# Layer 3's self attention: values and sums one turn earlier in the software pipeline

## The chip, the cores and the metric

The kernel runs on one core of a Trainium2 chip. The metric is the device time of one execution in microseconds; times are given as the median over runs. TensorE (PE in the profile, PEld its weight loads), VectorE (DVE), ScalarE (ACT) and GpSimd (POOL) each run their own instructions in order and wait for each other by semaphores.

## The reference

The program is a decoder of four layers, each a token mixer, a cross attention and a feed-forward part, each followed by a residual and a layer norm. It works on 16 sequences of 128 tokens with 256 channels. The change touches only the token mixer of layer 3, a self attention with 16 heads of 16 channels and a penalty on each pair of positions:

```python
def _L3_attn_ref(hidden_states, Wq, bq, Wk, bk, Wv, bv, Wg, bg):
    ...
    log_pen = jnp.log(jnp.maximum(penalties, 1e-32))
    ...
    q = split_heads(hidden_states @ Wq + bq)
    k = split_heads(hidden_states @ Wk + bk)
    v = split_heads(hidden_states @ Wv + bv)
    scores = jnp.einsum('bhqd,bhkd->bhqk', q, k) / np.sqrt(HEAD_DIM)
    scores = scores + log_pen[:, None, :, :]
    probs = jax.nn.softmax(scores, axis=-1)
    ctx = jnp.einsum('bhqk,bhkd->bhqd', probs, v)
    ctx = ctx.transpose(0, 2, 1, 3).reshape(b, s, h)
    return ctx
```

The result is added to x and layer-normalised: `x = _layernorm(x + _L3_attn_ref(...))`.

## The kernel before

The kernel holds the 16 blocks of 128 tokens (one sequence each, NB = 16) in SBUF from stage to stage. One function, `attention16`, serves four attentions: the cross attentions of layers 1, 2 and 3 and the self attention of layer 3. Only the last passes a `penalty` (a table of weights by which the exponentials are multiplied), and `own=True` (keys and values come from x itself). Its buffers appear in the profile with the prefix `a_` (and those of layer 3's cross attention, which follows it, with `x_`).

The function is a software pipeline written out by hand. Every engine runs over the same `TURNS`, n = -1, 0, 1, ...; in each turn it works on several blocks at different depths, and a block's number is n minus a fixed distance. `LAG` is the distance of the values and sums (`attend_values`, `attend_sums`), and the steps behind them stand at LAG + 1, LAG + 2 and LAG + 3. With the penalty LAG is 2, without it 1. In turn n, for layer 3's self attention:

- TensorE: `scores(n, 0)` (scores of block n, first half of the heads, for the maxima, in pR; interleaved with the scores of block n-1, second half, the right way round for the exponentials, in pT), `turn_back(n-LAG-3)`, `output(n-LAG-2)` (transposes for this attention), `scores(n, 1)`, `projections(n+1)`, `maxima(n)` (two transposes of the maxima), `attend_values(n-LAG)` and `attend_sums(n-LAG)` (32 matmuls each, line 2073).
- ScalarE: the exponentials of block n-1 (both halves), the copy of the turned-back x, then queries, value and key of block n+1.
- VectorE: `maximum(n, 0)`, `residual(n-LAG-2)`, `normalise(n-LAG-1)`, `maximum(n, 1)`, `put_maxima(n)` (the maxima go into spare rows of the queries; it waits for TensorE's `maxima(n)`), `spread(n-LAG-2)`, then the two weighings `weigh(n-1, 1)` and `weigh(n-1, 0)` (exponentials times penalty, line 2265), and `scaled(n-LAG-2)`.
- GpSimd: adds the bias to the values of block n+1 and writes them to a buffer of V; the power of the norm, the store of x and the residual's copy.

`attend_values(b)` waits for both weighings of block b:

```python
def attend_values(b):
    since(pe, w_done[0], b)
    since(pe, w_done[1], b)
    since(pe, v_stored, b)
    since(pe, oT_ready, b - 1)
```

`since(eng, event, b)` waits until the event has happened for block b. With LAG = 2 those are the weighings that VectorE did in the turn before. V has LAG + 2 buffers; the weights Pr have two (block parity).

Of the kernel before, what the change touches and what calls it, by code (L numbers as in the profile page):

```python
# [1838 lines left out]
def attention16(core, a, name, early, bq=False, bv=False, bo=False, own=False, rope=False, mask=None, penalty=None,  # L1839
# [3 lines left out]
    with Stage(core, name) as s:  # L1843
        SCALE = float(DH) ** -0.5
        LIFT = 60.0
        SLOTS16 = KD * PAIR
        LAG = 2 if penalty is not None else 1
        TURNS = range(-1, NB + LAG + 3)
        KV = core.XT if own else core.CT
        moved = bq and not rope  # L1850
# [24 lines left out]
        kx = [s.sb(f"kx{i}", [P, SLOTS16, P]) for i in range(4)]  # L1875
        V = [s.sb(f"V{i}", [P, H16, ROWS]) for i in range(LAG + 2)]
        mx = s.sb("mx", [P, KD, P])
# [42 lines left out]
        def live(b):  # L1920

            return 0 <= b < NB
# [17 lines left out]
        def _(pool):  # L1940
# [13 lines left out]
            def sum_k(b):  # L1954
                since(pool, k_turned, b)
                since(pool, k_stored, b - 1)
                pool.tensor_tensor(k32[:], rk[0][:], rk[1][:], ALU.add).then_inc(k_summed, 1)
# [7 lines left out]
            def residual(b):  # L1965
                since(pool, y_used, b - 1)
                if bo:
                    pool.tensor_tensor(xres[:], core.X[:, b, :], bot[:], ALU.add).then_inc(xres_ready, 1)
                else:
                    pool.tensor_copy(xres[:], core.X[:, b, :]).then_inc(xres_ready, 1)  # L1970

            def root(b):
                since(pool, ve_ready, b)
                pool.tensor_tensor(rstd[:], ve[:], core.mhalf[:], ALU.pow).then_inc(rstd_ready, 1)  # L1974

            def store(b):
                since(pool, xn_ready, b)
                pool.tensor_copy(core.X[:, b, :], xn[:]).then_inc(x_stored, 1)

            for n in TURNS:  # L1980
# [4 lines left out]
                if rope and live(n + 1):  # L1985
                    sum_k(n + 1)
                if live(n - LAG - 2):
                    root(n - LAG - 2)
                    store(n - LAG - 2)
                if live(n - LAG - 1):  # L1990
                    residual(n - LAG - 1)
# [340 lines left out]
def l1_xattn(core, a, after):  # L2332
    attention16(core, a, "x1", core.x1, bq=True, bv=True, bo=True, rope=True, after=[*after, core.a2])
# [38 lines left out]
def l2_xattn(core, a, mask, lists, values):  # L2372
    attention16(core, a, "x2", core.x2, bo=True, mask=(mask.out, mask.back), after=[lists, core.a3, core.pen],
                kv=(core.keys2, values))


def l3_xattn(core, a, tables, values):
    attention16(core, a, "x3", core.x3, bo=True, after=[tables], kv=(core.keys3, values))
# [1838 lines left out]
```

## Time and profile before

| | |
|---|---|
| median of 3 runs | 2903.16 us (2898.19 to 2906.47) |
| the profiled execution | 2894.84 us, of which the span of the trace is 2892.9 us |
| granted TensorE clock, mean over the span | 0.914 |
| TensorE, VectorE, ScalarE, GpSimd busy | 83%, 49%, 29%, 23% of the span |
| the stage of layer 3's self attention | from about 2154 to 2345 us |

The profile lists instructions with the line of the kernel, what they write and read, and the idle time of the engine ahead of them with what released it. The granted clock is the share of TensorE's full 2.4 GHz that it was given; 0.50 is 1.2 GHz.

### The profile page before, as it was taken

The numbers are of one execution on the slowest core, as the hardware profiler recorded it, in microseconds if no ns is written. First come the engines' busy times: TensorE is split into PE (matmuls) and PEld (weight loads), VectorE is DVE, ScalarE is ACT, GpSimd is POOL, SyncE is SP. The second block draws the span as 40 slices with busy tenths as digits, with TensorE's granted clock in tenths as the row PEclk, the third lists the DMA queues.
The fourth block names the chain that finished last, engine by engine and source line by source line (L and its number), as shares of the span: only waits on it lengthen the run. The fifth ranks groups of instructions, "written<-read, shape, count | busy, mean of one in ns | idle before, by whom it ended". The sixth has DMA issues, their size and how long they took to land. (4 is left out here: it accounts for less than half of the span.)

```text
span 2892.9 us, 53588 instructions
## 1 busy us (share of the span) xinstructions
PE 2415.0 (83%) x20563; PEld 1900.2 (66%) x20565; DVE 1421.9 (49%) x2899; ACT 847.3 (29%) x1462; POOL 676.6 (23%) x1011
## 2 busy tenths in 40 slices
PE   7869999568889899899889979729887869499990
PEld 3847777334578665799778856518656657399980
DVE  3256666576458631121267747551167958611115
ACT  1123333453234311011122224302245525122220
POOL 1932222231123200122112201102212212123331
PEclk8979999888989999999999989959889979799995
DMA  9020000100020000688500020015400000289982
GB/s 339 6 78 1 0 0 1 30 0 0 1 83 2 31 1 0 254 311 322 199 16 0 0 81 2 31 45 146 129 1 2 3 4 3 90 286 325 325 278 89
DMA packets 163710, 254.27 MB, mean 88 GB/s; under 512 B 17760, under 2 KB 124512, under 8 KB 163296
## 3 DMA queue, kind: packets, MB, share of 16 engines
q1 hardware_dynamic: 154336, 230.98, 23.1%
q0 software_dynamic: 9216, 21.06, 2.7%
q8 instruction: 114, 1.87, 0.3%
q14 instruction: 44, 0.36, 0.0%
HBM read 220.35 MB, written 31.13 MB: 87 GB/s over the span
## 5 line engine op out<-in xcount | busy, mean ns | idle before, releaser
L3180 PE MATMUL te_pU<-te_xsT,te_wu 128*128 128x128 f32 x1952 | 235.6, 278 | 1.6 <-DVE te_xsT L3260 1.6
L3180 PEld LDWEIGHTS te_pU<-te_xsT,te_wu 128*128 128x128 f32 x1952 | 233.0, 195 | 5.4 <-issue 2.4
L3201 PE MATMUL te_pY<-te_wd,te_hT 128*128 128x256 f32 x976 | 220.8, 379 | 0.0
L3201 PEld LDWEIGHTS te_pY<-te_wd,te_hT 128*128 128x128 f32 x976 | 180.7, 190 | 22.0
L2252 DVE TENSOR_REDUCE x_mx<-x_pR 128x8 f32<-128x1024 f32 x96 | 117.4, 1223 | 74.5 <-PE x_pR L2042 71.5
L2167 ACT ACTIVATE x_Pr<-x_pT 128x1024 f32<-128x1024 f32 x96 | 97.9, 1020 | 169.5 <-PE x_pT L2047 169.5
L1117 PE MATMUL x_pB<-early,x_xlT 128*128 128x384 f32 x384 | 137.5, 502 | 4.7 <-DVE x_qn L1344 3.0
L2042 PE MATMUL x_pR<-x_kx,x_qx 32*128 32x128 f32 x1536 | 118.4, 293 | 22.3 <-ACT x_kx L2200 13.8
L2042 PEld LDWEIGHTS x_pR<-x_kx,x_qx 32*128 32x128 f32 x1536 | 100.3, 196 | 51.2 <-issue 45.8
L3221 ACT ACTIVATE te_hT<-te_pU 128x512 f32<-128x512 f32 x78 | 46.6, 597 | 242.4 <-PE te_pU L3180 242.4
L2047 PE MATMUL x_pT<-x_qx,x_kx 32*128 32x128 f32 x1536 | 115.6, 289 | 1.4 <-ACT x_Pr L2167 1.2
L3239 DVE COPY te_ys<-te_pY 128x256 f32<-128x256 f32 x61 | 25.9, 425 | 162.8 <-PE te_pY L3201 162.8
L3234 DVE TENSOR_TENSOR te_hT<-te_pU,te_sg 128x512 f32<-128x512 f32 x44 | 30.4, 692 | 149.4 <-ACT te_sg L3219 149.4
L1117 PEld LDWEIGHTS x_pB<-early,x_xlT 128*128 128x128 f32 x384 | 71.1, 195 | 47.8 <-issue 5.4
L3219 ACT ACTIVATE te_sg<-te_pG 128x512 f32<-128x512 f32 x44 | 26.3, 597 | 251.4 <-PE te_pG L3180 251.4
L2047 PEld LDWEIGHTS x_pT<-x_qx,x_kx 32*128 32x128 f32 x1536 | 96.9, 192 | 3.2 <-ACT x_Pr L2167 1.7
L3236 DVE COPY te_xsT<-te_pT 128x256 f32<-128x256 f32 x61 | 25.7, 421 | 134.5 <-PE te_pT L3174 134.5
L1974 POOL TENSOR_TENSOR x_rstd<-x_ve,mhalf 128x1 f32<-128x1 f32 x48 | 26.3, 549 | 277.6 <-DVE x_ve L2291 277.6
L3180 PE MATMUL te_pG<-te_xsT,te_wg 128*128 128x128 f32 x704 | 86.0, 275 | 0.0
L2301 DVE RECIPROCAL x_R<-x_pO 128x256 f32<-128x256 f32 x48 | 83.9, 1748 | 0.5 <-PE x_pO L2073 0.5
L3180 PEld LDWEIGHTS te_pG<-te_xsT,te_wg 128*128 128x128 f32 x704 | 82.5, 193 | 0.0
L2000 PE MATMUL x_pq<-XT,early 128*128 128x128 f32 x512 | 78.1, 308 | 5.2 <-PEq L284 3.0
(618 smaller groups left out, 5601.3 us busy)
## 6 DMA issues: line engine op xcount, KB each, us to landing
te_wu<-in_L_ffn_w_upT SPq DMA_DIRECT2D x39, 1024.0 KB, 5.6
te_wd<-in_L_ffn_w_downT SPq DMA_DIRECT2D x39, 1024.0 KB, 5.7
te_wu<-in_L_ffn_up SPq DMA_DIRECT2D x22, 1024.0 KB, 5.0
te_wg<-in_L_ffn_gate SPq DMA_DIRECT2D x22, 1024.0 KB, 7.0
te_wd<-in_L_ffn_down SPq DMA_DIRECT2D x22, 1024.0 KB, 7.8
moe_first<-in_L_ffn_W SPq DMA_DIRECT2D x8, 1024.0 KB, 8.6
ao_got<-ys_slots SPq DMA_DIRECT2D x12, 512.0 KB, 6.1
xs_slots<-zeros SPq DMA_DIRECT2D x1, 5120.0 KB, 23.5
```

Of the source, the lines that this page charges most:

```text
L1117: ins = pe.matmul(pB[:, n, 0:HALF], xlT[t][:, src + k, :], w[:, k, bass.ts(n, HALF)], start=(k == 0), stop=(k == KD - 1))
L1974: pool.tensor_tensor(rstd[:], ve[:], core.mhalf[:], ALU.pow).then_inc(rstd_ready, 1)
L2000: ins = pe.matmul(out[:, t, :], ws[t // KD][:, k, bass.ts(t % KD, P)], src[:, k, bass.ts(b, P)], start=(k == 0), stop=(k == KD - 1))
L2042: return pe.matmul(pR[:, j, c, :], qx[b % 4][g, c, :], kx[b % 4][g, c, :], start=mask is None, stop=mask is None or c == SLOTS16 - 1)
L2047: return pe.matmul(pT[:, j, c, :], kx[b % 4][g, c, :], qx[b % 4][g, c, :], start=mask is None, stop=mask is None or c == SLOTS16 - 1)
L2167: ins = act.activation(Pr[b % 2][half][:], pT[:], ACT.Exp, scale=SCALE)
L2252: dve.tensor_reduce(out, pR[:].rearrange("p j (i t) n -> p (j i) t n", i=PAIR), AX.X, ALU.max).then_inc(mx_ready[half], 1)
L2301: dve.reciprocal(R[:], pO[:, 1, :, :]).then_inc(o_inverted, 1)
L3180: ins = pe.matmul(out[g][:, m, :], w[:, k, bass.ts(PER * g + m, P)], xsT[:, k, :], start=(k == 0), stop=(k == KD - 1))
L3201: ins = pe.matmul(pY[u][:, 0, :], hT[:, k, :], wd[u][:, k, :], start=(k == 0), stop=(k == KH - 1))
L3221: act.activation(hT[:, PER * g:PER * (g + 1), :], pU[g][:], act_fn).then_inc(h_done, 1)
L3234: dve.tensor_tensor(hT[:, PER * g:PER * (g + 1), :], pU[g][:], sg[g][:], ALU.mult).then_inc(h_done, 1)
```

## The change

LAG is 1 for every caller. In layer 3's self attention the values and sums of a block are then asked for in the turn in which VectorE weighs its exponentials (block n-1 in turn n), output, residual, normalising and turning back come one turn sooner, V has three buffers instead of four, and the loop has one turn less (n goes to 19 instead of 20). The order of the steps within a turn is unchanged on every engine, as are all computations. The other three attentions stay the same.

```diff
-        LAG = 2 if penalty is not None else 1
+        LAG = 1
         TURNS = range(-1, NB + LAG + 3)
```

## Rows read from the trace of the kernel before

**Rows 1.** Busy time by windows: engine busy us (instructions), granted clock, DMA share, GB/s

```profile
core 0: us, PE busy (x) PEld busy (x) DVE busy (x) ACT busy (x) POOL busy (x), PEclk, DMA share, GB/s
2154.00:2345.30 191.30, 143.18 (x2464) 122.37 (x2464) 145.34 (x213) 92.27 (x192) 47.43 (x70) 0.91 0.01 2
2172.40:2182.90 10.50, 7.01 (x86) 6.24 (x86) 4.53 (x5) 5.40 (x11) 0.72 (x1) 0.84 0.01 2
...
2223.70:2309.95 86.25, 72.84 (x1386) 62.22 (x1386) 79.39 (x118) 51.99 (x109) 26.43 (x36) 1.00 0.01 2
...
2312.40:2315.40 3.00, 0.00 (x1) 0.01 (x1) 2.89 (x3) 1.11 (x1) 0.00 (x0) 1.00 0.01 3
2315.90:2319.30 3.40, 3.40 (x67) 2.93 (x66) 3.18 (x6) 0.00 (x0) 1.46 (x1) 0.56 0.00 0
...
2327.70:2331.10 3.40, 0.03 (x1) 0.00 (x0) 3.00 (x5) 0.22 (x1) 0.12 (x1) 0.71 0.00 0
```

**Rows 2.** Timeline of VectorE, one steady turn: start us, us

```profile
2242.89 1.22 DVE L2252 TENSOR_REDUCE a_mx<-a_pR 128x8 f32<-128x1024 f32 x1
...
2247.04 1.22 DVE L2252 TENSOR_REDUCE a_mx<-a_pR 128x8 f32<-128x1024 f32 x1
2248.80 0.88 DVE L2259 SCALAR_TENSOR_TENSOR a_qx<-a_pX,place,a_qx 128x256 f32<-128x256 f32 x2 [0.55 <-PE a_pX L2105]
...
2249.88 2.35 DVE L2265 TENSOR_TENSOR a_Pr<-a_Pr,early 128x1024 f32<-128x1024 f32 x2
...
2252.47 1.22 DVE L2252 TENSOR_REDUCE a_mx<-a_pR 128x8 f32<-128x1024 f32 x1
```

**Rows 3.** Timeline of TensorE, end of the same turn and start of the next

```profile
2248.36 0.41 PE L2105 MATMUL a_pX<-ident,a_mx 128*128 128x128 f32 x2 [0.18 <-issue]
2248.70 1.08 PE L2073 MATMUL a_pO<-a_Pr,a_V 128*32 128x128 f32 x32
2249.59 1.06 PE L2073 MATMUL a_pO<-a_Pr,ones_half 128*32 128x128 f32 x32
2250.60 0.35 PE L2042 MATMUL a_pR<-a_kx,a_qx 32*128 32x128 f32 x1
```

**Rows 4.** Timelines of TensorE and VectorE in turns 0 to 3

```profile
2160.96 1.27 PE L2042 MATMUL a_pR<-a_kx,a_qx 32*128 32x128 f32 x16 [2.04 <-ACT a_kx L2197]
2163.61 2.08 PE L2042 MATMUL a_pR<-a_kx,a_qx 32*128 32x128 f32 x16 [1.39 <-DVE a_mx L2252]
...
2172.43 0.34 PE L2042 MATMUL a_pR<-a_kx,a_qx 32*128 32x128 f32 x1 [2.20 <-ACT a_kx L2197]
...
2173.65 1.23 DVE L2252 TENSOR_REDUCE a_mx<-a_pR 128x8 f32<-128x1024 f32 x1 [2.50 <-PE a_pR L2042]
...
2181.61 2.88 DVE L2265 TENSOR_TENSOR a_Pr<-a_Pr,early 128x1024 f32<-128x1024 f32 x2
2184.42 1.21 DVE L2252 TENSOR_REDUCE a_mx<-a_pR 128x8 f32<-128x1024 f32 x1
...
2195.17 1.22 DVE L2252 TENSOR_REDUCE a_mx<-a_pR 128x8 f32<-128x1024 f32 x1
...
2201.51 3.09 DVE L2265 TENSOR_TENSOR a_Pr<-a_Pr,early 128x1024 f32<-128x1024 f32 x2
```

**Rows 5.** Timelines of TensorE, VectorE and ScalarE in the last turns

```profile
2315.98 1.94 PE L2073 MATMUL a_pO<-a_Pr,a_V 128*32 128x128 f32 x32
...
2319.26 1.16 PE L2047 MATMUL a_pT<-a_qx,a_kx 32*128 32x128 f32 x16
...
2331.18 1.94 PE L2073 MATMUL a_pO<-a_Pr,a_V 128*32 128x128 f32 x32 [3.45 <-DVE a_oT L2304]
...
2317.16 2.35 DVE L2265 TENSOR_TENSOR a_Pr<-a_Pr,early 128x1024 f32<-128x1024 f32 x2
...
2324.34 2.35 DVE L2265 TENSOR_TENSOR a_Pr<-a_Pr,early 128x1024 f32<-128x1024 f32 x2
...
2344.84 0.37 ACT L2216 COPY XT<-a_pX 128x256 f32<-128x256 f32 x1 [3.31 <-PE a_pX L2112]
```

**Rows 6.** Groups of instructions by line in the stage: busy us, mean ns

```profile
L1945 POOL MEMSET a_V<- 128x512 f32 x4 | 1.9, 533 | 0.0
```

## The prediction

> **What bounds the kernel now.** The reading goes from the whole to one turn. The span and the instructions of the function's buffers show where layer 3's self attention lies, the windows what it takes [rows 1]: the stage takes 191.3 us of the 2892.9 us span, from 2154.0 to 2345.3. No other stage is touched, because only this call of the function has a penalty; every other call already has a LAG of 1. So the question is what 191 us become.
>
> In the nine steady turns that follow 2223.7 VectorE is busy for 79.39 of 86.25 us and TensorE for 72.84, at a granted clock of 1.00 [rows 1]. VectorE is the bound, and its timeline of one turn shows why [rows 2]. The first maximum starts at 2242.89, the second at 2247.04; after a short wait for TensorE's transposes the maxima are put into the queries at 2248.80; the two weighings run from 2249.88 for 2.35 us, so to 2252.23; the next turn's first maximum starts at 2252.47. That is 9.34 us from first maximum to the end of the weighings, 0.24 us more to the next first maximum, and a turn of 9.58 us. TensorE stands beside this, not in it [rows 3]: it turns the maxima at 2248.36, at once goes on with values and sums (2248.70 to 2250.60, 1.90 us), and starts the next turn's scores at 2250.60, while VectorE still weighs. The next scores are finished before VectorE asks for them. What makes this possible is that the values and sums of this turn use weights that VectorE finished one turn ago.
>
> **The change, part by part.**
>
> Values and sums of block n-1 are now asked for in turn n, the turn in which VectorE weighs that block. VectorE's order isn't changed: its weighings stand behind the second maximum and behind put_maxima, which waits for TensorE's turned maxima of the same turn. TensorE's queue is in order: behind its wait for both weighings stand the 64 matmuls of values and sums, then the next turn's scores; and for those scores VectorE's next first maximum waits. What lay side by side becomes one chain:
>
> - from the end of the weighings to TensorE's first matmul behind its wait: 0.10 us (second maximum ends at 2248.26, transposes start at 2248.36) [rows 2, 3]
> - values and sums: 1.90 us [rows 3]
> - scores until the first maximum can start: 1.22 us, from turn 1, where VectorE did wait for them (2172.43 to 2173.65) [rows 4]
>
> The sum is 3.22 us from the end of the weighings to the next first maximum, where there were 0.24: 2.98 us more for each turn, a turn of 9.34 + 3.22 = 12.56 us. That the other 9.34 us stay rests on this: everything between first maximum and weighings is released from the scores or the first maximum, in the same order; and what is now a turn "younger" (the output of block n-3, its residual, the normalising of block n-2) has its inputs from the turn before, as it had. VectorE now stands idle for some 2.9 us of each turn behind the last scaling, and TensorE from about the turned maxima to the end of the weighings: 2248.36 + 0.41 to 2252.33, about 3.5 us.
>
> The turns one by one. Turn 1 has the first weighing; it ends at 2181.61 + 2.88 = 2184.49, the next first maximum moves from 2184.42 to 2184.49 + 3.22 = 2187.71, which is +3.29 [rows 4]. Turn 2 gets its first normalising, which turn 3 had; turn 3 took 9.43 us from first maximum (2195.17) to the end of the weighings (2201.51 + 3.09), so turn 2 becomes 9.43 + 3.22 = 12.65 in place of 10.75: +1.90 [rows 4]. The 12 turns from 3 to 15 give 12 x 2.98 = +35.8. By the first maximum of turn 15 the stage is 41.0 us late.
>
> The end gains a little. Before, turn 15's weighings end at 2317.16 + 2.35 = 2319.51 and turn 16's at 2324.34 + 2.35 = 2326.69, 7.18 us later; the scores of turn 16 had begun at 2319.26, 7.43 us ahead of that end [rows 5]. Now these scores start 0.10 + 1.90 = 2.00 us after 2319.51's counterpart: 9.43 us in place of 7.18, +2.25. Then the last values and sums, which began at 2331.18, 4.49 us after the last weighing, since they stood one turn deeper, begin 0.10 us after it: -4.39 [rows 5]. What follows them (to the last copy into XT at 2344.84) is the same work. So -2.1 in all: the turn saved is a drain turn, not a full one.
>
> The value buffer less costs nothing: each write to V waits for the sums of three blocks back instead of four, and the distance in turns to those sums is the same. One memset of 0.53 us goes from GpSimd's start [rows 6], off the path, since ScalarE's first work waits for the first projections as well. It could give 0.5 us at the most.
>
> At full clock the sum is 3.3 + 1.9 + 35.8 - 2.1 = **+38.9 us**.
>
> **The clock** is the unknown term. TensorE gets a pause of some 3.5 us in each turn, right ahead of the matmuls that now are on the path. Before, the steady turns leave TensorE 86.25 - 72.84 = 13.4 us in nine turns, 1.5 us a turn in several pieces, and the clock stays at 1.00 [rows 1]. At the end there are two that long: after the one from 2312.4 to 2315.4 the values and sums ran at 0.56 of the clock, and in the one from 2327.7 to 2331.1 it fell (0.71 over that stretch) [rows 1]. At 1.2 GHz values and sums took 2315.98 to 2319.26, 3.28 us, so 1.38 more than at 2.4 GHz [rows 3, 5]; sixteen score matmuls took 2.08 instead of 1.27, 0.81 more [rows 4]. So a turn costs between 0 (the clock holds) and 2.2 us more (both slow). Turn 1, with a pause of 2.20 us ahead of its scores, has a mean clock of 0.84 [rows 1, 4], so the clock falls and comes back within one turn, and I don't expect it to fall on each of the new ones: I take three in four of 15 turns (the sixteenth, the last, ran slow before too), at 1.4 us: +16 us. The ends are 0 and 15 x 2.2 = +33.
>
> For a loop in which TensorE waits between bursts, the Trainium skill ("TensorE: Matmul & The Clock Gate", section "HAM oscillation — how this bites in real kernels") warns that each burst can start at the lower clock. Taken for every turn, values and sums alone, that would be 15 x 1.4 = +21 and +60 in all. Two of two such pauses here agree with it; the steady turns show no pause of that length, so they don't test it.
>
> Total: 38.9 + 16 = **+55 us** on the profiled execution's 2894.8 (span 2892.9), which gives 2950. The runs shown have a median of 2903.16, 8.3 above the profiled one; I put the same 55 on the median: **2958 us**.
>
> **Rivals.**
> - The clock holds (0.20). For it: some 9 us of a turn in which TensorE is as busy as before. Against it: both pauses of this length. Time 2903 + 39 = 2942.
> - The clock falls in every turn and is still low in the scores (0.25). For it: both bursts that followed such a pause were slow. Against it: the sixteen scores behind the first, from 2319.26, took only 1.16 us, so the clock was back for them [rows 5]. 39 + 33 = 72: 2975. The rule of the Trainium skill named above speaks for this one.
> - Not slower, the one on the other side (0.03): the wait is hidden, because TensorE comes to it late. It would need TensorE's arrival (2248.70) to slip behind the end of the weighings (2252.23), so 3.5 us of delay in projections or maxima that costs VectorE nothing; from there on only the drain's gain is left: 2903 - 4 = 2899. VectorE's put_maxima waits for those same transposes, so a delay there moves the weighings with it; I see nothing that gives it.
> - The forecast, most but not all pauses with a fall: 0.50. The other 0.02 are cases that I don't see.
>
> **Numbers.** From the first two rivals and the clock's bounds, less 4 us for the spread of the runs at the low end, the range is 2938 to 2975. A difference of 0.3% is 9 us, about what a measurement can tell; faster than that 0.01, within it 0.03, slower 0.96.
>
> **What the profile afterwards would show.** A first-maximum period of 12.6 us at full clock and about 14 with a fall; VectorE idle for some 3 us before the first maximum, released by the scores; TensorE idle for 3.5 us ahead of values and sums, released by the weighings; a mean granted clock of the stage below 0.91; the stage some 245 us long and all others as they were. Wrong would be: a period near 9.6 (the wait hidden); more than 14.8 (a second wait that I missed, in projections or keys); or a clock of 1.00 through the steady turns (the term of 16 us gone).

## The result and the profile after

| | before | after |
|---|---|---|
| median | 2900.7 us (4 runs) | 2964.3 us (2960.4 to 2968.4, 4 runs) |
| ratio | 1 | 1.0214, 95% interval 1.0197 to 1.0231 |
| span of the profiled execution | 2892.9 us | 2958.5 us |
| mean granted clock | 0.914 | 0.907 |

The four runs before are the three shown ahead and one more. The kernel is 2.1% slower: some 62 us by the ratio, 63.6 by the medians. The forecast was 2958 (2938 to 2975). "Turn n" is below the time from the first maximum of block n to that of block n+1. Of the 65.6 us between the two spans, 61.6 lie in the stage of layer 3's self attention: from VectorE's first instruction there to its last scaling it takes 250.83 us (2157.84 to 2408.67) instead of 189.27 (2154.38 to 2343.65). The stage begins 3.5 us later in this execution; in the other profiled executions below, in which nothing ahead of it differs either, it begins anywhere from 2152.7 to 2161.7, so that part isn't the change's.

The windows after, with the same columns as [rows 1]: the stage, the eleven turns from 2219.3 on, a pause and what followed it, and another pause and what followed it.

```profile
2157.80:2409.20 251.40, 162.99 (x2463) 139.34 (x2463) 145.76 (x212) 90.54 (x191) 47.37 (x69) 0.83 0.01 1
2219.30:2375.90 156.60, 108.06 (x1695) 92.31 (x1696) 98.02 (x144) 62.28 (x132) 32.15 (x44) 0.86 0.01 2
2282.35:2285.85 3.50, 0.00 (x0) 0.00 (x0) 3.43 (x7) 1.75 (x6) 2.18 (x2) 1.00 0.02 5
2285.80:2289.40 3.60, 3.54 (x68) 3.15 (x68) 0.34 (x2) 0.00 (x0) 0.74 (x2) 0.53 0.00 0
2324.30:2327.80 3.50, 0.00 (x0) 0.00 (x0) 3.44 (x7) 1.74 (x6) 2.18 (x2) 0.88 0.00 0
2327.80:2332.50 4.70, 4.70 (x84) 4.09 (x88) 0.27 (x1) 0.00 (x0) 0.74 (x2) 0.50 0.02 3
```

VectorE's busy time in the stage is what it was (145.76 us, 145.34 in [rows 1]); it does the same work, spread over more time, and the clock of the steady turns is 0.86 where it was 1.00. In the first of the two pauses shown the clock was still at 1.00 and fell as TensorE started again; in the second it fell near the pause's end (0.88). One turn on VectorE's timeline, which answers to [rows 2]:

```profile
2276.46 1.23 DVE L2252 TENSOR_REDUCE a_mx<-a_pR 128x8 f32<-128x1024 f32 x1 [4.45 <-PE a_pR L2042]
...
2280.62 1.22 DVE L2252 TENSOR_REDUCE a_mx<-a_pR 128x8 f32<-128x1024 f32 x1
2282.39 0.88 DVE L2259 SCALAR_TENSOR_TENSOR a_qx<-a_pX,place,a_qx 128x256 f32<-128x256 f32 x2 [0.55 <-PE a_pX L2105]
...
2283.46 2.35 DVE L2265 TENSOR_TENSOR a_Pr<-a_Pr,early 128x1024 f32<-128x1024 f32 x2
2285.72 0.41 DVE L2297 TENSOR_SCALAR a_xn<-a_r,a_mv,a_rstd 128x256 f32<-128x256 f32 x1
2290.59 1.23 DVE L2252 TENSOR_REDUCE a_mx<-a_pR 128x8 f32<-128x1024 f32 x1 [4.46 <-PE a_pR L2042]
```

From the first maximum to the end of the weighings (2285.81) there are 9.35 us, as before (9.34). Behind them stands a wait that [rows 2] don't have: 4.46 us until TensorE's scores. TensorE's timeline of the same turn, which answers to [rows 3]:

```profile
2281.94 0.41 PE L2105 MATMUL a_pX<-ident,a_mx 128*128 128x128 f32 x2 [0.16 <-issue]
2285.86 1.86 PE L2073 MATMUL a_pO<-a_Pr,a_V 128*32 128x128 f32 x32 [3.52 <-DVE a_Pr L2265]
2287.47 1.96 PE L2073 MATMUL a_pO<-a_Pr,ones_half 128*32 128x128 f32 x32
2289.36 0.38 PE L2042 MATMUL a_pR<-a_kx,a_qx 32*128 32x128 f32 x1
```

TensorE stands for 3.52 us after the turned maxima, released by the weighing (L2265); then values and sums take 2285.86 to 2289.36, 3.50 us at 0.53 of the clock instead of 1.90, and only then come the scores. Not every fall comes this early. Two turns sooner the values still ran at full speed behind the same pause, and only the sums were slow:

```profile
2257.62 1.08 PE L2073 MATMUL a_pO<-a_Pr,a_V 128*32 128x128 f32 x32 [3.51 <-DVE a_Pr L2265]
2258.52 1.78 PE L2073 MATMUL a_pO<-a_Pr,ones_half 128*32 128x128 f32 x32
```

The waits, added up from 2219 to 2376 (us in total, times, longest), show both halves of this ring:

```profile
DVE a_mx L2252 <- PE a_pR L2042: 54.4, 12, 5.4
PE a_pO L2073 <- DVE a_Pr L2265: 38.7, 11, 3.5
```

Neither wait stands in the same list of the steady turns before (2219 to 2310).

### The profile page after: what moved, and what is told of

Its sections match the earlier page's. It is cut to its first block and busy times, and to the rows that moved or that the text cites. A ratio compares the mean times of both kernels' runs of the same rounds, so it can differ in the third digit from the quotient of the medians.

```text
span 2958.5 us, 53589 instructions
## 1 busy us (share of the span) xinstructions
PE 2437.3 (82%) x20563; PEld 1921.2 (65%) x20565; DVE 1422.3 (48%) x2899; ACT 846.2 (29%) x1462; POOL 676.8 (23%) x1010
## 3 DMA queue, kind: packets, MB, share of 16 engines
q8 instruction: 114, 1.87, 0.3%
## 5 line engine op out<-in xcount | busy, mean ns | idle before, releaser
L2042 PE MATMUL x_pR<-x_kx,x_qx 32*128 32x128 f32 x1536 | 118.8, 294 | 22.5 <-ACT x_kx L2200 13.8
```

The source lines that it names most:

```text
L2042: return pe.matmul(pR[:, j, c, :], qx[b % 4][g, c, :], kx[b % 4][g, c, :], start=mask is None, stop=mask is None or c == SLOTS16 - 1)
```

## The experiments

Each is timed beside the kernel before on the same chip; ratios are to it, and a difference between two of these kernels is one of ratios, with 1% as 29 us, unless medians are named. "Stage" is, as above, the profiled execution's time from VectorE's first instruction in the stage to its last scaling (before 189.3 us, after 250.8).

| kernel | ratio, 95% interval | steady turn, us | clock there | stage, us |
|---|---|---|---|---|
| before (LAG 2) | 1 | 9.58 | 1.00 | 189.3 |
| after (LAG 1) | 1.0214 (1.0197 to 1.0231) | 13.8 to 15.1 | 0.86 | 250.8 |
| e1_filler | 1.0199 (1.0183 to 1.0214) | 13.84 | 1.00 | 248.1 |
| e1b_filler14 | 1.0120 (1.0100 to 1.0141) | 12.51 | 1.00 | 225.4 |
| e2_lag2_v3 | 1.0085 (1.0069 to 1.0100) | 9.0 to 13.4 | 0.87 | 213.8 |
| e3_lag1_v4 | 1.0213 (1.0193 to 1.0233) | 13.8 to 15.1 | 0.83 to 0.89 | 252.8 |
| e4_weigh_first | 1.0086 (1.0071 to 1.0102) | 11.33 or 12.95 | 1.00 or 0.87 | 221.8 |
| e10_weigh_first_filler | 1.0044 (1.0029 to 1.0059) | 11.33 | 1.00 | 204.3 |
| e6_noweigh_lag1 | 0.9953 (0.9937 to 0.9968) | 8.96 | 1.00 | 172.8 |
| e7_noweigh_lag2 | 0.9972 (0.9960 to 0.9985) | 8.96 | 1.00 | 181.3 |
| e5_lag2_split | 0.9995 (0.9985 to 1.0004) | 9.47 | 1.00 | 189.8 |
| e8_lag2_spread_first | 1.0009 (0.9997 to 1.0021) | 9.04 | 1.00 | 187.2 |
| e11_v3_root_first | 0.9990 (0.9980 to 1.0000) | 9.58 | 1.00 | 190.5 |

### How much of it is the clock

The first try keeps TensorE busy in its pause with matmuls whose results are overwritten.

```diff
             def attend_values(b):
+                if penalty is not None:
+                    since(pe, oT_ready, b - 1)
+                    for i in range(22):
+                        pe.matmul(pO[:, 0, i % KD, :], core.ident[:], wq[:, 0, 0:P], start=True, stop=True)
                 since(pe, w_done[0], b)
```

> The changed kernel, with 22 more fp32 matmuls of 128x128 by 128 columns in TensorE's queue between the turned maxima and the wait for the weighings, of constant data into a part of pO that the values overwrite. At 1.16 us for 8 such matmuls they take 3.1 us of a pause of 3.6 us, so they delay nothing, but TensorE is busy in it. Theory (the wait costs 2.98 us a turn, and the rest of the 62 us is the clock's fall in each pause): the granted clock is 1.00 in the steady turns, a turn takes 12.6 us, and the kernel is 39 us slower than the one before (2940). Rival (the rest is a cost of the chain itself, not of the clock): a turn stays at 14.1 us and the kernel at 2964.

Measured: the clock is 1.00, as expected, but the time hardly moves (1.0199). The expectation had the filler's size wrong: 22 of them take 5.08 us, not 3.1, and push values and sums back. The profile counts an fp32 matmul as two records (22 matmuls are x44), and 3.1 us had been worked out from the projections' x8 in 1.16 us as if these were eight. TensorE's timeline:

```profile
2243.91 1.08 PE L2073 MATMUL a_pO<-a_Pr,a_V 128*32 128x128 f32 x32
...
2252.74 5.08 PE L2082 MATMUL a_pO<-early,ident 128*128 128x128 f32 x44
```

The weighings there ended at 2242.52 (they start at 2240.17 and take 2.35), so the values came 1.4 us late. By the next run, whose turn is 1.33 us shorter at the same clock, it is this delay that took the place of the low clock. So this run doesn't tell the theory from its rival by its time. It was repeated with `range(14)`.

> As the filler before, with 14 instead of 22 extra matmuls. There 22 took 5.08 us (0.23 each), held the clock at 1.00 and pushed values and sums 1.3 us behind the end of the weighings, in a turn of 13.84 us; 14 take 3.2 us and end ahead of it. Theory (the wait costs 2.98 us a turn, the rest is the clock): a turn of 12.55 us, clock 1.00 in the steady turns, 39 us slower than the kernel before (2941). Rival (the extra 1.5 us a turn belong to the chain, whatever the clock): 14.1 us a turn, 2964.

```profile
2239.73 1.23 DVE L2256 TENSOR_REDUCE a_mx<-a_pR 128x8 f32<-128x1024 f32 x1 [2.84 <-PE a_pR L2042]
...
2246.73 2.35 DVE L2269 TENSOR_TENSOR a_Pr<-a_Pr,early 128x1024 f32<-128x1024 f32 x2
...
2252.24 1.23 DVE L2256 TENSOR_REDUCE a_mx<-a_pR 128x8 f32<-128x1024 f32 x1 [2.84 <-PE a_pR L2042]
```

```profile
2245.46 3.29 PE L2082 MATMUL a_pO<-early,ident 128*128 128x128 f32 x28
2249.14 1.08 PE L2073 MATMUL a_pO<-a_Pr,a_V 128*32 128x128 f32 x32 [0.39 <-DVE a_Pr L2269]
```

The first fence is VectorE's timeline of a turn, the second TensorE's. TensorE still waits 0.39 us for the weighing, so the filler delays nothing; the turn takes 12.51 us (2239.73 to 2252.24), and there are 3.16 us from the end of the weighings (2249.08) to the next first maximum, against 3.22 worked out in the prediction. More work on TensorE makes the changed kernel 27 us faster by the ratios, 30 by the medians (2934.0 against 2964.3). What is left, 1.2% or 35 us, stands with the clock at 1.00 through the steady turns: the price of the wait alone. The run shows that a low clock made up the rest; 27 to 30 us are what the matmuls gave back, and 25.4 by the two stages (250.8 and 225.4).

### The value buffer, and the depth

```diff
-        V = [s.sb(f"V{i}", [P, H16, ROWS]) for i in range(LAG + 2)]
+        V = [s.sb(f"V{i}", [P, H16, ROWS]) for i in range(3)]
```

In the kernel before, that is three buffers at LAG 2:

> The kernel before (LAG 2) with three buffers of V instead of four: one part of the change alone. Theory (the buffer plays no part in the change's time): nothing of the 62 us comes from it. At LAG 2, though, GpSimd's write of block n+1's values then waits for the sums of block n-2, which end in the same turn some 1.4 us after that write began before, and the root of the norm stands behind it: with 0.65 us of slack that may delay the scaling by 0.7 us a turn, so 0 to +9 us. Rival (the buffer is the cause of a good part): +20 us or more.

Measured: 1.0085, 24 us slower. That is past the 9 us of the theory and where the rival had put it, so at LAG 2 the missing buffer costs. Whether it costs in the change is a question for LAG 1. The converse is four buffers at LAG 1 (`LAG + 3` with a penalty):

> The changed kernel (LAG 1) with four buffers of V: the turn of depth alone. The write of block n+1's values waits for sums of one or two turns before, in either case long done. Theory: the same as the changed kernel within 3 us (2964, 1.021). Rival (the missing buffer costs here too, as it did at LAG 2, where it cost 24 us): faster than the changed kernel by 10 us or more.

Measured: 1.0213 beside the changed kernel's 1.0214, each known to 0.2%. So the buffer plays no part in this change that these runs can see (2.4 us by the medians), and the turn of depth is the whole of it. It is the combination that counts: with as many buffers as LAG + 1, the write of new values waits for sums of its own turn; with LAG + 2 it waits for older ones. In the three-buffer run at LAG 2 the waits of the eleven turns from 2208 on say where it went:

```profile
POOL a_V L1962 <- PE a_pO L2073: 97.6, 12, 9.8
...
PEld a_pX L2112 <- DVE a_xn L2297: 19.0, 10, 2.1
DVE a_qx L2259 <- PE a_pX L2105: 18.5, 11, 3.3
```

GpSimd's write now waits for the sums. The root behind it comes late, and with it VectorE's scaling (2244.15 in one turn, with 0.44 us of waiting for the root). TensorE waits 1.5 to 1.9 us a turn for that ahead of turning back; its clock over these turns is 0.87; and VectorE waits for the turned maxima for up to 3.3 us. To test the first link, the write was moved behind GpSimd's root, store and residual copy, still with three buffers at LAG 2:

> LAG 2 with three buffers of V, and GpSimd's write of the values moved behind its root, store and residual copy. Theory (in the run with three buffers at LAG 2 that write, waiting for the sums of its own turn, held up the root behind it, so the scaling, so TensorE's turning back, and that pause made the clock fall): the write's wait now holds up nothing, a turn is back at about 9.6 us, clock 1.00, and the kernel within 5 us of the one before. Rival (the buffer's wait reaches the path by the values themselves): still 20 us slower.

Measured: 0.9990, turns of 9.58 us, clock 1.00. With the write behind it the root is on time and the cost is gone, so the late root was what brought the write's wait to the path. How the 24 us split between that delay and the clock wasn't tried. An estimate from the run itself: in four of its eleven turns from 2208.78 to 2338.49 the clock doesn't fall, and these take 10.65 to 10.71 us, some 1.07 more than before, so about 12 us of delay over the eleven; the other 12 would be the clock's.

### Where the weighings stand

LAG 1, with both weighings ahead of put_maxima:

```diff
+                if penalty is not None and live(n - 1):
+                    weigh(n - 1, 1)
+                    weigh(n - 1, 0)
                 if live(n):
                     put_maxima(n)
                 if live(n - LAG - 2):
                     spread(n - LAG - 2)
-                if penalty is not None and live(n - 1):
-                    weigh(n - 1, 1)
-                    weigh(n - 1, 0)
```

> The changed kernel (LAG 1), with both weighings ahead of put_maxima in VectorE's order instead of behind it. Theory (what costs is where the weighings stand in VectorE's queue): from first maximum to the end of the weighings 7.7 us instead of 9.34, and 3.2 us from there to the next first maximum at full clock, so a turn of 10.9; TensorE's pause shrinks to about 1.9 us, the clock should mostly hold. 13 turns x 1.3 us - 2 us of drain = +15 us against the kernel before, up to +30 if the clock falls in some turns (2916 to 2931). Rival (the wait is for something else, values or normalising): no gain on the changed kernel, 2964.

Measured: 1.0086, 25 us slower than before and 37 us (1.3%) faster than the changed kernel. The same depth costs far less when VectorE reaches the weighings sooner. The rival (no gain) is out, and the time lies in the expected range, but the quick turns take 11.33 us and not 10.9. The weighings end 8.17 us after the first maximum and not 7.7, because the two took 2.88 us here (from 2234.16) instead of 2.35; the second ran for 1.75 us, with GpSimd's write of the values on it (0.77 us from 2235.19). In turn 1 of the kernel before, where such a write lies on the pair too, they took 2.88 as well [rows 4]; whether the overlap is the reason wasn't tried. The turns are of two kinds, and the windows of one of each differ in TensorE alone:

```profile
2228.90:2240.20 11.30, 8.03 (x155) 6.87 (x155) 9.40 (x13) 5.68 (x12) 2.06 (x4) 1.00 0.01 2
2240.20:2253.10 12.90, 9.63 (x155) 8.25 (x156) 9.44 (x13) 5.67 (x12) 2.07 (x4) 0.87 0.01 3
```

The same 155 matmul records take 8.03 us at 1.00 and 9.63 at 0.87, the turn 1.6 us more; VectorE's 13 instructions take the same. The pause of 2.34 us ahead of the values is the same in both, and the clock is at 1.00 all through it in both: in the second it fell at about 2248.7, behind the start of the values (2248.43). Eight of the twelve turns from block 3 to 15 are of the slow kind; what picks them isn't shown. With six extra matmuls in the pause:

> LAG 1 with both weighings ahead of put_maxima, and 6 extra matmuls (1.4 us) in TensorE's pause of 2.3 us ahead of the values. Without them the turns took 11.33 us or 12.95 us, by whether the clock had fallen in the pause. Theory (the clock makes the second kind): all steady turns take 11.33 us at a clock of 1.00, about 12 us faster than without the extra matmuls, so 14 us slower than the kernel before (1.005). Rival (the two kinds come from something else, such as GpSimd and VectorE together): still two kinds, 1.009.

Measured: all steady turns 11.33 us, clock 1.00, ratio 1.0044 where 1.005 was expected. So here too the second kind of turn is the clock's. The other half of the ring, values and sums behind the next turn's scores in TensorE's queue, was left as it is in every run.

### Without the weighings

The multiplication of the exponentials by the penalty is left out, and values and sums wait for the exponentials, at LAG 1 and at LAG 2.

```diff
-        w_done = [s.sem(f"w_done{i}") for i in range(2)] if penalty is not None else e_done
+        w_done = e_done
...
-                if penalty is not None and live(n - 1):
-                    weigh(n - 1, 1)
-                    weigh(n - 1, 0)
```

> LAG 1 without the two weighings (the exponentials aren't multiplied by the penalty), values and sums waiting for the exponentials alone. Theory (the wait for the weighings is the change's cost): values and sums follow the turned maxima at once, a turn takes about 9.0 us, bound by TensorE's queue, and the kernel is 7 to 10 us faster than the one before, and 2 to 6 us faster than the next one. Rival (the shorter depth itself costs): slower than its LAG 2 partner by 10 us or more.

> LAG 2 without the two weighings: the partner of the run ahead. Theory: a turn of about 9.0 us too, with one drain turn more, so 2 to 6 us slower than the LAG 1 partner. Rival: 10 us or more faster than the partner.

Measured: 2885.6 and 2889.9 us, both with most steady turns at 8.96 us (three of LAG 1's at 9.3 to 9.6, one of LAG 2's at 9.4) and the clock at 1.00. LAG 1 comes out 4 us ahead, within the 2 to 6 expected, though the intervals (0.9937 to 0.9968 and 0.9960 to 0.9985) overlap. So without the weighings the shallower pipeline costs nothing, and may give the drain turn. The pair doesn't isolate the wait: the weighings' 2.35 us leave VectorE's turn too, and GpSimd's root takes 0.55 us instead of 1.46. That it is the wait for the weighings that costs rests on this pair together with the wait rows after the change and the run with the weighings first. Against the kernel before LAG 1 gained 13.6 us by the medians, where 7 to 10 were expected.

### A version that beats both?

The kernel before waits 0.55 us in each turn for the turned maxima. LAG 2, with the first weighing in that wait:

```diff
+                if penalty is not None and live(n - 1):
+                    weigh(n - 1, 1)
                 if live(n):
                     put_maxima(n)
                 if live(n - LAG - 2):
                     spread(n - LAG - 2)
                 if penalty is not None and live(n - 1):
-                    weigh(n - 1, 1)
                     weigh(n - 1, 0)
```

> The kernel before (LAG 2), with the first of the two weighings ahead of put_maxima, in the 0.55 us in which VectorE waits for the turned maxima. Theory (VectorE is the bound of the steady turn and 0.55 us of it is that wait): a turn of 9.03 to 9.1 us instead of 9.58, over 12 to 13 turns 6 to 7 us faster than the kernel before (0.997 to 0.998), as long as the maxima are put in by 2250.6, when TensorE ends its sums. Rival (TensorE's queue is the bound in truth): no gain, or slower since the queries come 1.2 us later.

Measured: 0.9995, turns of 9.47 us, only 0.11 us less. Of the 0.55 us of waiting, 0.44 came back at the scaling, further down the queue:

```profile
2243.18 1.22 DVE L2265 TENSOR_TENSOR a_Pr<-a_Pr,early 128x1024 f32<-128x1024 f32 x1
2244.84 0.41 DVE L2297 TENSOR_SCALAR a_xn<-a_r,a_mv,a_rstd 128x256 f32<-128x256 f32 x1 [0.44 <-POOL a_rstd L1974]
```

With `spread` ahead of the first weighing as well:

> The kernel before (LAG 2) with VectorE's order changed: spread, first weighing, put_maxima, second weighing. The earlier try without spread in front gained only 0.1 us a turn (9.47), since the root on GpSimd then came 0.44 us too late for the scaling. Theory: with the variance ready one step sooner that wait goes too, a turn of 9.0 to 9.1 us, 12 x 0.5 = 6 us faster than the kernel before (0.998), and faster than both kernels of the change. Rival (TensorE's own queue is the next bound at once): 9.4 us a turn, no difference.

Measured: turns of 9.04 us, as expected, and no gain: 1.0009, 0.9997 to 1.0021. In the profiled execution eleven turns (first maxima of blocks 4 to 15, 2211.26 to 2310.90) save 5.8 us against before, but the four ahead of them take 44.2 us (2167.11 to 2211.26) instead of 42.2, and the rest of the stage 35.6 instead of 33.7; the stage ends 2.1 us shorter, and the median doesn't show it. No version that still weighs is faster than the kernel before by more than the noise.

## Why the prediction was right, point by point

- **The new ring** (weighings, values and sums, scores, first maximum): right. Worked out at 3.22 us from the end of the weighings to the next maximum at full clock; 3.16 in the run with the filler, in a turn of 12.51 us against 12.56.
- **The other 9.34 us stay**: right, 9.35.
- **Turn 1**: +3.29 worked out. It takes 14.03 us (2177.05 to 2191.08), before 10.77, so +3.26, and that agreement is luck. The working kept the 10.84 us that VectorE had needed before from first maximum to the end of the weighings, in a turn whose clock had fallen to a mean of 0.84 [rows 1]. After the change the clock doesn't fall there and the same part takes 9.25 us (to 2186.30); it falls behind the new pause instead. With the filler turn 1 takes 12.42 us, so at full clock the change costs it 1.65 and not 3.29.
- **Turn 2**: +1.90 worked out. It takes 14.28 (to 2205.36) against 10.75, +3.53 with the clock in it; with the filler 12.62, +1.87. Right.
- **The twelve turns from 3 to 15**: +35.8 worked out at full clock; the filler run has +35.4 (150.14 us against 114.78). Right. With the clock they took 170.53 us (2205.36 to 2375.89), +55.75, so 20 of these 56 us are the clock's, 1.7 a turn.
- **The end**: -2.1 worked out. From the first maximum of turn 15 to the last scaling there are 32.78 us instead of 33.70, -0.9 with the slow clock in it, and 31.03 in the filler run, -2.7.
- **The sum at full clock**, +38.9: the stage of the filler run is 36.2 us longer than before, its median 35 us higher. Of the 2.7 us too much, turn 1 makes 1.6 and the end 0.6.
- **The clock**: the term whose size was off. "Three in four of 15 turns at 1.4 us", +16; measured 25.4 by the stages with and without the filler, and 27 to 30 by the times. Both factors were too low: the clock fell in every turn, and a fall cost 1.7 us in the mean. The rival with each turn slow had the count right. In ten of the twelve turns the clock was back by the next first maximum (waits for the scores of 4.1 to 4.5 us); in the two others (15.1 us, waits of 5.4) it stayed at 0.50 through values, sums and scores, as from 2327.80 on above. These two lie beyond the 2.2 us that the prediction took as the most, and beyond the 14.8 us that it named as the sign of a second wait; there was none. The pause that decides was seen rightly; that it would let one turn in four pass was a guess from turn 1, whose pause is shorter and sits elsewhere.
- **The total**: the stage took 61.6 us more and not 55. A clock term 9.4 too low and a sum at full clock 2.7 too high partly cancel, so the forecast is nearer than its largest uncertain term. The mechanism was right.
- The rule in the Trainium skill ("TensorE: Matmul & The Clock Gate", section "HAM oscillation — how this bites in real kernels"), that a loop with waits between its bursts can start each one at the lower clock, agrees with these traces in the count: the clock was low behind the 3.5 us pause in every turn, and in the steady turns before it never was. It agrees less in the place: at 2257.62 and 2342.92 the burst began at full speed (values in 1.08 us), and the fall came within it.
- **The value buffer costs nothing**: right at LAG 1, for the reason given (the distance in turns stays the same).
- **Not slower** and **the clock holds**: both excluded, by the waits of 3.52 us at L2073, the turns of 13.8 to 15.1 us and the clock of 0.86.

## What to carry to other kernels

The distance between a step and its consumer in a software pipeline must be counted in queue positions, not in turns: a consumer may stand in the same turn only if the producer stands early enough in its engine's order. Here moving the producer ahead of one wait was worth 37 us of the 62, and even then 25 were left. Price a new wait of TensorE at the clock as well as at its length: matmuls put into the pause, of no use otherwise, gave back nearly half of the loss, and too many of them next to nothing. A buffer count is tied to the depth: one too few shows up not at the buffer but at what stands behind its wait in the same queue.

## What was not expected of the hardware

- In the kernel before the clock held at 1.00 through turns with some 1.5 us of pauses. With a pause of 1.5 to 1.9 us ahead of turning back (three buffers at LAG 2) it fell in seven of eleven turns; with one of 2.34 us ahead of the values in 8 of 12; with one of 3.5 us in all. It often fell only behind the pause, when TensorE was at work again: 2282.35 to 2285.85 at 1.00, then 0.53 to 2289.40.
- Extra matmuls made a kernel faster: 14 a turn, 3.3 us of TensorE work, some 27 us in all.
- An fp32 matmul stands in the profile as two records. The "64 matmuls" of values and sums and the "sixteen score matmuls" of the prediction (and the 32 a part of the section on the kernel) are such records, of half as many instructions in the program; the durations, and so the sum, are not touched by it.
